# A decoder block on one core: statistics moved out of two openings, the last normalization and the store moved into the last stage

## The reference, cut to what matters

```python
x = x + attn(_layernorm(x))                  # gated delta rule, 16 key heads, 32 value heads
x = x + xattn(_layernorm(x), ctx, mask)      # cross-attention, 16 heads of 16 channels, 512 x 512
x = x + ffn(_layernorm(x))                   # silu(x W1) * (x W3), Walsh-Hadamard transform, W2

def _layernorm(x, axis=-1, eps=1e-05):
    m = jnp.mean(x, axis=axis, keepdims=True)
    v = jnp.var(x, axis=axis, keepdims=True)
    return (x - m) / jnp.sqrt(v + eps)
```

## Time and profile before

| | us |
|---|---|
| median of 3 runs | 4097.15 |
| the profiled execution's own time | 4098.42 |
| its span | 4096.6 |
| PE busy | 3877.1 (95%) |
| DVE busy | 2923.3 (71%) |
| ACT busy | 2465.3 (60%) |
| POOL busy | 640.7 (16%) |

### The profile page before, as it was taken

The page is one execution under the profiler, slowest core; times in us unless marked ns, Lnnn a source line. Parts: engine busy times, 40 slices in busy tenths (PEclk is TensorE's granted clock), DMA queues, the critical chain, the costliest instruction groups (busy, mean ns, idle before and its releaser), DMA issues. The chain is left out here.

```text
span 4096.6 us, 69187 instructions
## 1 busy us (share of the span) xinstructions
PE 3877.1 (95%) x26288; PEld 2880.1 (70%) x26288; DVE 2923.3 (71%) x4960; ACT 2465.3 (60%) x4877; POOL 640.7 (16%) x585
## 2 busy tenths in 40 slices
PE   4999999999999999999999999996899999699998
PEld 2777777777777777777777777774454554488886
DVE  5788888888888888888888888885566666322222
ACT  2677777777777777777777777774355555211111
POOL 1000000000000000000000000001456655310110
PEclk8999999999999999999999999997899999899999
DMA  2010111001110101101010010100776674400001
GB/s 80 24 38 27 35 37 34 27 27 34 37 34 27 33 28 37 35 27 45 17 41 31 27 45 17 45 17 21 121 127 117 120 124 84 113 21 5 17 16 41
DMA packets 156290, 187.53 MB, mean 46 GB/s; under 512 B 13212, under 2 KB 96924, under 8 KB 155964
## 3 DMA queue, kind: packets, MB, share of 16 engines
q1 hardware_dynamic: 153916, 182.62, 19.2%
q10 hardware_dynamic: 2048, 0.53, 0.1%
HBM read 150.79 MB, written 29.62 MB: 44 GB/s over the span
## 5 line engine op out<-in xcount | busy, mean ns | idle before, releaser
L407 PE MATMUL pj<-xh,w_hi 128*128 128x512 f32 x1536 | 680.7, 443 | 8.7 <-DVE w_lo L769 8.5
L407 PE MATMUL pj<-xh,w_lo 128*128 128x512 f32 x1536 | 610.6, 397 | 0.0
L407 PE MATMUL pj<-xl,w_hi 128*128 128x512 f32 x1536 | 607.0, 395 | 0.0
L1078 POOL TENSOR_TENSOR silu_z<-silu_z,exp_z 128x512 f32<-128x512 f32 x128 | 191.2, 1514 | 2529.7 <-ACT exp_z L649 2529.7
L1613 DVE TENSOR_REDUCE row_max<-s 128x1 f32<-128x512 f32 x512 | 340.2, 686 | 201.9 <-PE s L1376 198.6
L1551 ACT ACTIVATE probs<-s 128x512 f32<-128x512 f32 x512 | 292.1, 594 | 253.2 <-PE s L1400 249.9
L407 PEld LDWEIGHTS pj<-xh,w_lo 128*128 128x128 f32 x1536 | 289.5, 188 | 61.2
L407 PEld LDWEIGHTS pj<-xh,w_hi 128*128 128x128 f32 x1536 | 291.1, 190 | 57.9 <-issue 15.1
L407 PEld LDWEIGHTS pj<-xl,w_hi 128*128 128x128 f32 x1536 | 292.2, 190 | 49.9 <-issue 15.1
L838 DVE SCALAR_TENSOR_TENSOR conv_v<-conv_in,conv_w_section,conv_v 128x512 f32<-128x512 f32 x384 | 288.1, 750 | 10.3 <-ACT conv_v L632 1.2
L629 ACT ACTIVATE conv_in<-pj 128x512 f32<-128x512 f32 x256 | 153.6, 600 | 198.2 <-PE pj L407 106.8
(11 more groups left out here) (259 smaller groups left out, 9770.7 us busy)
## 6 DMA issues: line engine op xcount, KB each, us to landing
w_raw<-in_w_in SPq DMA_DIRECT2D x128, 256.0 KB, 6.4
decays<-decay_by_head SPq DMA_DIRECT2D x64, 512.0 KB, 3.7
decays<-decay_by_head SPq DMA_DIRECT2D x64, 256.0 KB, 5.0
q_stack<-qk_parts SPq DMA_DIRECT2D x128, 128.0 KB
k_stack<-qk_parts SPq DMA_DIRECT2D x128, 128.0 KB
f_raw<-in_f_w SPq DMA_DIRECT2D x32, 256.0 KB, 2.7
x_all<-in_x SPq DMA_DIRECT2D x4, 1024.0 KB, 10.4
source<-in_ctx SPq DMA_DIRECT2D x8, 512.0 KB
```

The costliest lines, as they stand in the source:

```text
L407: mm = pe.matmul(pj[j % 2][:, :], a[:, j, k * P:(k + 1) * P], b[:, k, bp * WIN:(bp + 1) * WIN], start=(n == 0), stop=(n == 3 * KT - 1))
L1078: pool.tensor_tensor(sz[p][:, :], sz[p][:, :], ez[p][:, :], ALU.mult).then_inc(E["sz"].sem, 1)
```

## The change

- `row_stats` is gone. Inside `cross_attention` DVE takes the statistics of tiles 0 and 1 first (`dve_stats(0, 2)`), and those of the other 14 after unit 1's projections, ahead of the first row maxima. ACT makes `rstd` in two parts.
- SP loads three weights first, then mask and source, then the other five. PE starts on the three (`first_in`) and no longer waits there for rows of ones and `v_placed`; it does so after the 30 steps of LEAD. The rows of ones are issued behind the first stacks. ACT's blanking lies between its other work, and POOL's memset of `v_placed` behind its work on the masks.
- In unit u (u >= 2), at step 16, DVE takes `bn_stats` of tile u - 2 for the last normalization.
- The ln3 block is gone. `feed_forward` begins with the statistics of the last two tiles, the 16 `bn_aggr` and `rstd`; the first window of group 0 is written by hand with the normalization and the transposes of the four windows between its chunks, in the banks `f_acc`.
- SP issues weight pieces 0 and 1, then the first group of down weights, the other six pieces, and then the other three groups.
- SP stores each window of `x_all` when its last addition is done, inside the stage. The last block is gone.

The diff, cut (not shown: the removal of `row_stats`, of ln3's prefetch and of the last block; and that the first chunk's product `pe_down` waits for all 16 lower parts, `pe_up` of chunk 0 of window w for the window's own four):

```diff
         def _(sp):
-            for dst, key in ((wq[:, :, :], "x_wq"), ...  all eight ...):
-                sp.dma_start(dst, a[key]).then_inc(loaded, 16)
-            sp.wait_ge(blank, 2)
-            sp.wait_ge(blank_odd, 2)
-            for f in range(2):
+            def ones_row(f):
                 sp.dma_start(ks[f][R_MAX:R_MAX + 2, :, :]...).then_inc(ones_in, 16)
...
             def start():
+                weights(((wq[:, :, :], "x_wq"), (bqk[:, :, :], "x_bqk"), (wk[:, :, :], "x_wk")), first_in)
                 load_mask(0)
                 load(0, True)
+                weights(((wv[:, :, :], "x_wv"), (bv[:, :], "x_bv"), (sel[:, :], "x_sel"), (mcol[:, :, :], "mask_col"),
+                         (half[:, :], "x_half")), loaded)
                 for side in range(2):
                     parts(0, 0, side)
-                for e in range(2):
-                    stack(0, 0, e, None)
-                    stack_masks(0, 0, e)
+                stack(0, 0, 0, None)
+                sp.wait_ge(blank, 2)
+                stack_masks(0, 0, 0)
+                stack(0, 0, 1, None)
+                stack_masks(0, 0, 1)
+                ones_row(0)
                 for side in range(2):
                     parts(1, 1, side)
                 stack(1, 1, 0, None)
+                sp.wait_ge(blank_odd, 2)
                 stack_masks(0, 1, 0)
+                ones_row(1)
                 load_mask(1)
...
         def pe_start(pe):
-            pe.wait_ge(loaded, 16 * 8)
-            pe.wait_ge(ones_in, 32)
-            pe.wait_ge(zeroed, 2)
+            pe.wait_ge(first_in, 16 * 3)
             pe_queries(pe, 0, 0, 0)
             pe_keys(pe, 0, 0, 0)
+            pe.wait_ge(loaded, 16 * 5)
             pe_source_values(pe, 0, 0)
...
                     pe_turn_max(pe, 0, n // 8 - 1)
+            pe.wait_ge(ones_in, 32)
+            pe.wait_ge(zeroed, 2)
...
         def act_start(act):
+            act_rstd(act, 0, 2)
+            act_blank(act, qs[1])
+            for i in range(2):
+                act_part(act, 0, i)
+            act_blank(act, ks[1])
+            for i in range(2):
+                act_part(act, 1, i)
+            act_rstd(act, 2, TILES)
...
         def dve_start(dve):
+            dve_stats(dve, 0, 2)
             dve_target(dve, 0, True)
+            dve.wait_ge(first_in, 16 * 3)
             for i in range(2):
                 dve_masked(dve, 0, 0, 0, i)
+            dve.wait_ge(loaded, 16 * 5)
             dve_source_values(dve, 0, 0)
             for i in range(2):
                 dve_masked(dve, 1, 0, 1, i)
+            dve_stats(dve, 2, TILES)
             for n in range(LEAD):
                 dve_maximum(dve, 0, n)
...
+                if n == 16 and u >= 2:
+                    E["x"].wait(dve, u - 2, 0)
+                    dve.bn_stats(out_stats[:, u - 2, :], x_all[:, u - 2, :]).then_inc(out_stats_done, 1)
...
             pool.wait_ge(blank, 2)
+            for i in range(2):
+                pool_rest(pool, 0, i)
+            pool.wait_ge(loaded, 16 * 5)
+            pool_mask(pool, 0, True)
             for f in range(2):
                 pool.memset(vz[f][:, :, :, :], 1.0).then_inc(zeroed, 1)
...
 feed_forward, SP:
-            load(0, True)
-            for g in range(2, GROUPS):
+            load(0, range(2))
+            load_down(sp, 0)
+            load(0, range(2, 2 * FG))
+            for g in range(1, GROUPS):
                 load_down(sp, g)
             for g in range(1, GROUPS):
-                load(g, False)
+                load(g, range(2 * FG))
+            for w in range(NW):
+                E["out"].wait(sp, (GROUPS - 1) * NW + w, 3)
+                sp.dma_start(out_v[:, 4 * w:4 * w + 4, :], x_all[:, 4 * w:4 * w + 4, :]).then_inc(stored, 16)
+            sp.wait_ge(stored, 16 * NW)
 feed_forward, PE:
+            def first_window():
+                pe_turn(pe, 0)
+                for c in range(3):
+                    pe_up(pe, 0, 0, 0, c)
+                    pe_turn(pe, c + 1)
+                pe_down(pe, 0, 0, 0)
+                pe_down(pe, 0, 0, 1)
+                pe_up(pe, 0, 0, 0, 3)
+                pe_down(pe, 0, 0, 2)
+                pe_up(pe, 0, 1, 1, 0)
+                pe_down(pe, 0, 0, 3)
 feed_forward, ACT:
+            upper_parts(0)
+            slice_(0, 0)
+            upper_parts(1)
+            slice_(0, 1)
+            upper_parts(2)
+            upper_parts(3)
+            slice_(0, 2)
+            slice_(0, 3)
 feed_forward, DVE:
+            for i in range(TILES - 2, TILES):
+                dve.bn_stats(stats[:, i, :], x_all[:, i, :]).then_inc(stats_done, 1)
+            dve.wait_ge(stats_done, TILES)
+            for i in range(TILES):
+                dve.bn_aggr(mv[:, i, :], stats[:, i, :]).then_inc(mv_done, 1)
+            dve.wait_ge(rstd_done, 1)
+            normalize(0)
+            lower_parts(0)
+            normalize(1)
+            hidden(0, 0)
+            lower_parts(1)
+            normalize(2)
+            hidden(0, 1)
+            lower_parts(2)
+            normalize(3)
+            lower_parts(3)
+            hidden(0, 2)
+            hidden(0, 3)
+            outputs(0, 0)
```

More of the change, by code:

```diff
@@ L1106, in _ @@
             run(dve, dve_prologue, dve_section, dve_epilogue)
[L1109 to L1135, removed]
 XS, XH, XD = 256, 16, 16
@@ L1836, in _, with pe_turn @@
                 split(g, False)
+        def pe_turn(pe, w):
+            for u in range(4):
+                i = 4 * w + u
+                pe.wait_ge(normed, i + 1)
+                if w:
+                    pe.wait_ge(lo_done, i - 3)
+                for k in range(KT):
+                    mm = pe.transpose(acc[u][:, k * P:(k + 1) * P], xn[u][:, k * P:(k + 1) * P], cols["ident"])
+                mm.then_inc(turned, 1)
         def pe_up(pe, g, r, w, c):
+            if g == 0 and c == 0:
+                pe.wait_ge(lo_done, 4 * (w + 1))
             if w == 0:
@@ L1871, in group @@
             def group(g, last):
-                for w in range(NW):
+                for w in range(0 if g else 1, NW):
                     r = g * NW + w
@@ L1903, in _, with slice_ @@
-            for r in range(GROUPS * NW):
-                slices(r)
+            def slice_(r, c):
+                E["gp"].wait(act, r, c)
+                if c:
+                    E["hlo"].wait(act, r, c - 1)
+                else:
+                    E["hlo"].wait_before(act, r)
+                act.activation(sg[:, :], gp[c % 2][:, :], ACT.Silu).then_inc(E["sg"].sem, 1)
+                E["hid"].wait(act, r, c)
+                if c >= 2:
+                    E["down"].wait(act, r, c - 2)
+                else:
+                    E["down"].wait_before(act, r)
+                act.activation(h_hi[c % 2][:, :], hid[:, :], ACT.Copy).then_inc(E["hhi"].sem, 1)
@@ new lines, in upper_parts @@
+            def upper_parts(w):
+                for u in range(4):
+                    i = 4 * w + u
+                    act.wait_ge(turned, i + 1)
+                    act.activation(xh[:, :, i * P:(i + 1) * P], acc[u][:, :].rearrange("p (k t) -> p k t", k=KT), ACT.Copy)\
+                        .then_inc(hi_done, 1)
+            act.preload_act_table_set(LOG_EXP)
+            act.wait_ge(mv_done, TILES)
+            act.activation(lnv[:, :], mv[:, :, 1], ACT.Ln, bias=cols["ln_eps"]).then_inc(lnv_done, 1)
@@ L1906, in _ @@
+            act.wait_ge(lnv_done, 1)
+            act.activation(rstd[:, :], lnv[:, :], ACT.Exp, scale=-0.5).then_inc(rstd_done, 1)
+            upper_parts(0)
[6 more added lines that the diff above has]
+            slice_(0, 3)
+            for r in range(1, GROUPS * NW):
+                for c in range(FG):
+                    slice_(r, c)
         @block.vector
         def _(dve):
[L1908 to L1926 removed]
@@ L1927, in _, with normalize, lower_parts @@
-            for g in range(GROUPS):
-                group(g)
+            def normalize(w):
+                for u in range(4):
+                    i = 4 * w + u
+                    if w:
+                        dve.wait_ge(turned, i - 3)
+                    dve.tensor_scalar(xn[u][:, :], x_all[:, i, :], mv[:, i, 0:1], rstd[:, i:i + 1], ALU.subtract, ALU.mult)\
+                       .then_inc(normed, 1)
+            def lower_parts(w):
+                for u in range(4):
+                    i = 4 * w + u
+                    dve.wait_ge(hi_done, i + 1)
+                    dve.tensor_tensor(xl[:, :, i * P:(i + 1) * P], acc[u][:, :].rearrange("p (k t) -> p k t", k=KT),
+                                      xh[:, :, i * P:(i + 1) * P].bitcast(F32), ALU.subtract).then_inc(lo_done, 1)
@@ new lines, in outputs @@
+            def outputs(r, w):
+                E["down"].wait(dve, r, FG - 1)
+                E["out"].wait_before(dve, r)
+                for u in range(4):
+                    dve.tensor_tensor(x_all[:, 4 * w + u, :], x_all[:, 4 * w + u, :], acc[u][:, :], ALU.add)\
```

(9 more changed lines are left out.)

131 lines of the change are left out of this document (54 added, 77 removed).

## The result

The changed kernel takes 4051.19 us (median of 4 runs, 4050.63 to 4052.51), against 4097.90 us for the kernel before in the same comparison (4 runs, 4096.87 to 4099.4). The ratio is 0.9886, with a 95% interval of 0.9869 to 0.9903. That is 46.7 us less. The prediction said 4050.9 us, 46.3 less. The profiled execution took 4052.51 us, with a span of 4050.7.

A forecast was written before the change was run, and what follows sets the result against it. PE, busy for 95% of the span, was taken as the bound, its idle time as winnable: 16.9 - 1.0 + 22.0 + 8.4 = 46.3 us off 4098.42, and 1.27 less as a median, 4050.9 us; range 4043 to 4063.

The forecast's parts named there:

- Part 1: Opening of cross-attention: PE starts 18.35 us early, less 1.5 us of new wait for the ones: 16.9 us won.
- the worse bound: Opening: second `target` ends behind POOL's second memset at 2841.7, not 2839.4; PE starts 18.35 us early, not 20.7.
- From there the old chain follows unchanged to the first pass: Opening, after PE's start: steps keep their old times, so the first pass's first matmul is due 18.35 us earlier, at 2866.35.
- Part 2: Units, step 16: 14 statistics of 0.60 to 0.68 us fit DVE's 0.83 us idle; cost 1.0 us, bounds 0 and 9.5.
- Part 3: Normalization inside the feed-forward stage's first window: 28.5 - 6.0 - 1.7 + 1.2 = 22.0 us won.
- That is 28.5 us earlier: Feed-forward stage: PE's first gate matmul comes at 3516.7 and not at 3545.26.
- Part 4: Kernel's end: three quarters of the store lie under the last group's windows; 8.4 us won, bounds 7 and 9.
- DVE shows: Units and opening: 14 statistics cost 9.5 us, first row maxima 2 us late, ones 3: 4062.9 us; chance 0.10.
- late weights: Feed-forward's first window: weight pieces 2 to 7 come late, 5 us, and no clock gain: 4057.1 us; chance 0.10.
- It doesn't overlap: Feed-forward's first window: every hand-over is waited for, transposes cost about 18 us, not 7.7: 4062.4 us; chance 0.05.
- slower: Units: DVE's wait for tile u - 2 holds up row maxima and PE, from 3.9 us per unit: about 4106; chance 0.02.
- Everything fits and more: No port wait (2.3), no wait for ones (1.5), clock up at once (1.3): 4045.8 us; chance 0.09.

The follow-up runs named there:

- experiment 5: Changed kernel, but POOL's second long memset waits until DVE has written both target tiles: 4048.70 us, ratio 0.988.
- experiment 7: Changed kernel plus 60 identity transposes on PE before the queries and 18 before the last stage's first window: 4048.16 us, ratio 0.9879.
- experiment 2: Changed kernel, but all 16 statistics of the last normalization at the feed-forward stage's start, none in the units: 4056.92 us, ratio 0.9902.
- experiment 3: Changed kernel, but each of the four stores waits for the very last addition: 4059.46 us, ratio 0.9908.
- experiment 6: Changed kernel, but rows of ones issued before any stack, in empty queues, with ACT blanking `ks[1]` first: 4050.06 us, ratio 0.9883.
- experiment 8: Changed kernel with the edits of experiments 5, 6 and 7 together, 36 transposes in place of 60: 4042.15 us, ratio 0.9864.
- experiment 4: Changed kernel, but SP issues both rows of ones ahead of the first mask stack: 4054.12 us, ratio 0.9892.
- experiment 1: Kernel before with only the new opening of cross-attention; units, last normalization, feed-forward stage and store stay old: 4085.49 us, ratio 0.9972.

## Why the prediction was right

The time is met within 0.3 us, but not because each term was. The opening and the last stage brought 3.8 and 1.4 us less than forecast. The units came out 3.8 better, and the delta stage, which ended earlier in this run, 0.7. That these cancel is luck. What was right is the mechanism: each part gained by the path that was described, and in about the size.

**Part 1, the opening (16.9, measured 13.1 from the block's start).** The start of PE came nearly as worked out: 2841.40 against 2841.8, or 7.6 us from the block's start against 7.3, with the second `target` ending just behind the memset. Experiment 5 shows that the memset was the cause, and so the choice of the worse bound was right. Three steps after that were off.

- *"From there the old chain follows unchanged to the first pass"* failed. The keys took 3.78 us and not 1.98. In the old kernel the clock rose between the queries and the keys; now both lie at the lower level. Experiment 7 takes it away by keeping PE busy. This is 1.8 us, a term that the sum lacked.
- The mask rows before the first pass were waited for 10.36 us and not 9.47: 0.9 more. This is no cost of the change: with the same opening the wait was 9.24 and 9.25 us in experiments 2 and 3.
- The ones cost 2.0 us of delay between first pass and unit 0 (27.94 against 25.90), where I took 1.5. Mechanism and place were right: the rows of ones are what the wait names, and experiment 6 removes the wait.

That the 14 statistics just fit ahead of the first row maximum was right, and it is as close as was said. In the changed kernel DVE was ready 1.0 us before the first scores were there; in experiments 7 and 8, where the first pass came 5.0 and 6.6 us sooner, the statistics held the first maxima, and PE waited 0.8 us once and not 0.36.

The row of the kernel before that I should have carried over (its timeline, right behind the queries):

```profile
2864.75 1.98 PE L1337 MATMUL prep<-source,wk 128*128 128x512 f32 x4 [0.84 <-DVE q_full L1596]
```

The weights hid, as said, with 3 us to spare: when PE could start that much sooner, it waited for them, by 0.14 us in experiment 5 and about 1 us in experiment 8.

**Part 2, statistics in the units (-1.0, measured +2.8).** The idle 0.83 us of the earlier trace rows took them, as this timeline of the changed kernel shows. It is the same step as there:

```profile
3180.43 0.68 DVE L1663 BATCH_NORM_STATS2 ln_stats<-x_all 128x6 f32<-128x512 f32 x1
3181.03 0.68 DVE L1609 TENSOR_REDUCE row_max<-s 128x1 f32<-128x512 f32 x1
...
3181.94 2.18 DVE L1609 TENSOR_REDUCE row_max<-s 128x1 f32<-128x512 f32 x3 [0.23 <-PE s L1352]
```

No price shows: the shortest unit is 37.19 us long with the statistics (experiments 4 and 5) and without them (experiment 2). Nor is the gain of 2.8 us theirs, since experiment 1, with the old units, has 2.0 of it. Between the first and the last `recip_den` of the units lie 539.8 us in the trace of before and 538.8 in the one after, but 535.7 to 538.9 in the eight experiments. That is 1.0 of the 2.8; the other 1.8 lie in front of the first and behind the last. What differs are waits of PE for transfers, before and then after, over the units (us in total, times, longest):

```profile
PE prep L1337 <- DMA source<-in_ctx: 3.6, 5, 1.3
...
PE s L1400 <- DMA q_stack<-neg_max_lo: 1.7, 2, 0.8
```

```profile
PE prep L1313 <- DMA source<-in_ctx: 1.6, 3, 0.8
```

One unit of before was 38.97 us long and not 37.2, with a source load 1.3 us late in it. The trace of before is the longest of the ten between unit 0 and the last stage (597.7 against 592.8 to 596.8). It is the only one of its code, so it isn't shown whether it was a slow sample or whether the old opening left the queues later. A sum made against one profiled execution inherits that.

**Part 3, the feed-forward stage (22.0, measured 20.6).** The step that was off is *"That is 28.5 us earlier"*; it was 27.2. The term took the first transposes 3.7 us after the stage's start (they came after 3.8), but gave the four `ln_xn` no collision. Beside POOL's splits they took 4.15 us; alone they take 1.91 (experiment 2). In experiment 8 one of the four met no split (0.54 us in place of 1.48), and the gate came 8.8 us into the stage and not 9.8. I had used this very mechanism in part 1 and not here.

From the first gate matmul to the additions I had 41.46 + 6.0 + 1.7 - 1.2 = 47.96 us, and it took 48.10. The three rounds took 1.91 each (5.7 in all), and the wait of `pe_down` was 1.94. Together they are 7.67, so 7.67 - 6.64 = 1.0 us was given back elsewhere, where I had booked 1.2 for the clock. That this term fits is luck of the one trace. In experiments 3 to 6, the same code, the first 4 us behind the gate's start ran at 0.50 as in the kernel before (0.59 in the changed kernel), 48.5 to 49.2 us passed from the gate to the additions, and only 0 to 0.6 us was given back. Against their traces part 3 brought 19.4 to 20.1 us. With the clock at the upper level throughout, experiment 7 won another 1.46, which makes up the 2.5 us that I had as the upper bound.

The weights of later pieces were on time: PE's only waits until the additions are the first tiles, `fxl` and `pe_down`. The row of `pe_down` names no releaser, but it starts 0.11 us behind the last lower part, as forecast:

```profile
3524.23 2.48 DVE L1982 TENSOR_TENSOR fxl<-f_acc,fxh 128x512 fp32r<-128x512 f32 x4 [1.36 <-ACT fxh L1948]
```

**Part 4, the store (8.4, measured 8.6; 8.3 in experiment 3)** was right, and hidden under PE's work as said.

**The rivals.** "DVE shows" falls by experiment 2, and "late weights" by the absence of any such wait. "It doesn't overlap" falls by the 7.7 us that were to come back and did (1.91 x 3 + 1.94), and "slower" by units of unchanged length. "Everything fits and more" was excluded by the memset, the ones and the clock. Experiment 8 takes away the three costs that it names: it had 4045.8, and 4042.15 was measured, since it counted the clock with 1.3 us in the last stage alone, and the opening had another 3.6.

The Trainium skill's exclusive lock ("SBUF — State Buffer", SBUF: two separate sides) agrees with two places here: the queries start 3.3 us sooner when the second memset is out of the way, and the four `ln_xn` are 2.2 us shorter without POOL's splits. Its section Who interferes with whom adds that an instruction of VectorE with one SBUF input, outside the two-port modes, doesn't contend. The 14 statistics of the opening fit that: they ran at 0.60 us each (8.40 for 14) beside POOL's work on the mask.

## What to carry to other kernels

Once a start is pulled forward, walk the old chain again and ask of each step what its speed owed to the old moment: the clock that had time to rise, the port that was free, the queue that was empty. Each of these took back about 2 to 3 us in the opening, and each was won again by a small edit: a memset moved behind the tile it blocks, narrow transfers issued while the queue is empty, short transposes through a pause. And look at the spread of repeated units in the trace of before, and at more than one trace of the same code: a load that is late in one execution can show up as a false gain, and a clock level that holds in one as a term that fits.

## What the runs showed of the hardware

- A DVE `tensor_scalar` of 128x512 that met a memset of POOL over 64 partitions ended 0.28 us behind it: 3.81 us for the second tile, and 0.53 us when the memset was held back (5.31 and 2.03 us for the pair).
- Four such `tensor_scalar` beside POOL's casts and subtractions of 128x512 took 4.15 us, and 1.91 us without them. `bn_stats` beside POOL's work took 0.60 us each, as alone.
- In one trace two transfers of 32 KB into two partitions, put into a queue at work, delayed the transfer behind them by about 5 us. Issued while SP had nothing else to do, they showed no cost.
- Sixty transposes of a constant, 6.7 us in a pause of 8.9, held the upper clock level: the four query matmuls behind them took 1.96 us and not 3.75, and the granted clock was 1.0 and not 0.5.
- The level can fall behind a short pause, and doesn't do so in each execution. In the changed kernel PE idled 1.73 us before the first gate matmul, began it at 1.0 and ran at 0.52 from 3502 to 3504 without idle time; in experiment 7 the same pause was followed by 1.00. Behind the 1.94 us before `pe_down` the level fell to 0.50 in experiment 2 (3532 to 3534) and 0.52 in experiment 8, and stayed at 1.00 in the changed kernel and in experiment 7.
